# Five queues of the last attention put in another order, and ScalarE writing its transposed mask ahead of the score products

## What is computed

```python
# hidden_states, ssm_states: (8, 128, 256); 32 query heads, 8 key heads, head size 8
bias = concat([alibi, alibi], -1)            # slope[h] * (k - q)
mask = concat([0 <= q - k < 64, 0 <= q - k < 32], -1)
q = heads(concat([ssm_states, hidden_states], -1) @ Wq, 32)
k, v         = heads(hidden_states @ Wk, 8), heads(hidden_states @ Wv, 8)
ssm_k, ssm_v = heads(ssm_states @ Wsk, 8),   heads(ssm_states @ Wsv, 8)
kcat = concat([rep(ssm_k), rep(k)], 2); vcat = concat([rep(ssm_v), rep(v)], 2)
scores = q @ kcat.T / sqrt(8) + bias
scores = where(mask, scores, -inf)
o = softmax(scores) @ vcat
return o.reshape(B, T, 256) @ Wo
```

## Time and profile before

| | us |
|---|---|
| median of 3 runs | 1074.09 (1068.61 to 1078.88) |
| the profiled execution | 1076.21 |
| its span (first to last instruction) | 1074.40 |
| PE busy in the span | 988.4 (92%) |
| DVE, ACT busy | 639.3 (60%), 431.0 (40%) |
| stage E, t=9 to t=17 (from the first L800 to the last L1297) | 702.6 to 902.4 |

### The profile page before, as it was taken

One profiled execution on the slowest core, in us unless ns is written; L12 is line 12 of the kernel. 1 busy time (PEld: TensorE's weight loads), 2 busy tenths in 40 slices (PEclk: granted clock), 3 DMA queues, 4 the chain that ended last, 5 costly groups with the idle time before them and its releaser, 6 DMA issues.

```text
span 1074.4 us, 18672 instructions
## 1 busy us (share of the span) xinstructions
PE 988.4 (92%) x6076; PEld 775.9 (72%) x6076; DVE 639.3 (60%) x1450; ACT 431.0 (40%) x839; POOL 318.5 (30%) x534
## 2 busy tenths in 40 slices
PE   6999997979999999999999689867899998999994
PEld 5778885758888888888888335556677766688883
DVE  4676776535555555555556447665666673555555
ACT  4777783322323232232322123225555554422321
POOL 1132223224334434433444401110000004444331
PEclk9999997889999999999999779968999999999998
DMA  8000000553333333343330000011111101264511
GB/s 280 2 2 2 2 2 1 137 169 134 133 111 106 118 111 110 110 120 111 107 110 9 9 1 1 15 27 30 25 25 27 31 17 60 61 175 123 118 28 40
DMA packets 37354, 75.18 MB, mean 70 GB/s; under 512 B 7116, under 2 KB 18360, under 8 KB 37154
## 3 DMA queue, kind: packets, MB, share of 16 engines
q1 hardware_dynamic: 37006, 74.18, 23.8%
q0 software_dynamic: 288, 0.23, 0.2%
HBM read 67.21 MB, written 2.40 MB: 65 GB/s over the span
## 4 chain that ended last, share of the span: by engine, by line
PE 81%; DVE 6%; SPq 5%; issue 2%; DMA 2%; ACT 2%; POOL 1%; POOLq 0%; ACTq 0%; DVEq 0%
PE ps L1001 32%; PE ps L1018 15%; PE ps L413 4%; PE ps L638 4%; PE ps L502 3%; PE ps L420 3%; PE ps L867 2%; SPq L366 2%; SPq L322 2%; PE ps L494 2%; PE ps L533 2%; PE ps L755 1%; PE ps L805 1%; PE ps L846 1%; PE ps L842 1%
## 5 line engine op out<-in xcount | busy, mean ns | idle before, releaser
L1001 PE MATMUL ps<-shared 128*128 128x512 f32 x1560 | 383.3, 395 | 7.8 <-POOL shared L1999 7.1
L1001 PEld LDWEIGHTS ps<-shared 128*128 128x128 f32 x1560 | 296.9, 191 | 74.1 <-issue 12.2
L1405 ACT ACTIVATE shared<-pT 128x512 fp32r<-128x512 f32 x130 | 82.2, 632 | 286.3 <-DVE pT L1830 286.3
L1997 POOL CAST shared<-wraw 128x512 fp32r<-128x512 f32 (+1 forms) x130 | 91.3, 703 | 312.5 <-PE ps L1018 279.8
L1833 DVE TENSOR_TENSOR al<-pT,shared 128x512 fp32r<-128x512 f32 x130 | 116.8, 899 | 93.4 <-ACT shared L1405 93.4
L1822 DVE TENSOR_TENSOR e<-e,ps 128x512 f32<-128x512 f32 x130 | 89.4, 688 | 136.0 <-PE ps L1001 132.4
L1018 PE MATMUL ps<-shared 128*128 128x512 f32 x520 | 160.4, 390 | 1.3 <-DVE al L1833 1.2
L1999 POOL TENSOR_TENSOR shared<-wraw,shared 128x512 fp32r<-128x512 f32 (+1 forms) x130 | 132.1, 1016 | 10.4
L1887 POOL TENSOR_SCALAR newton<-agg 128x1 f32<-128x1 f32 (+1 forms) x36 | 9.2, 255 | 385.4 <-DVE agg L1450 358.8
L1018 PEld LDWEIGHTS ps<-shared 128*128 128x128 f32 x520 | 97.5, 188 | 22.8 <-DVE al L1833 2.1
L1399 ACT ACTIVATE e<-ps 128x512 f32<-128x512 f32 x130 | 77.7, 598 | 83.3 <-PE ps L1001 83.2
(11 more groups left out here) (222 smaller groups left out, 1429.2 us busy)
## 6 DMA issues: line engine op xcount, KB each, us to landing
kbd<-combine_C SPq DMA_DIRECT2D x46, 512.0 KB
wraw<-in_C_w SPq DMA_DIRECT2D x48, 384.0 KB, 8.1
kbd<-combine_F SPq DMA_DIRECT2D x15, 512.0 KB
wraw<-in_F_w SPq DMA_DIRECT2D x17, 384.0 KB, 7.0
kbd<-kbd SPq DMA_DIRECT2D x96, 32.0 KB, 1.9
kT<-kbd SPq DMA_DIRECT2D x48, 32.0 KB, 1.9
c_ctx_t<-in_ctx_t SPq DMA_DIRECT2D x1, 1024.0 KB, 8.6
out<-c_x_rows SPq DMA_DIRECT2D x2, 512.0 KB, 3.0
```

The costliest lines, as they stand in the source:

```text
L1001: mm = pe.matmul(GU[t][s], w[u][:, (c * 2 + s) * P:(c * 2 + s + 1) * P], xx[:, c, t * HALF:(t + 1) * HALF], start=(i == 0), stop=(i == 5))
L1405: act.activation(ah[t][:, :], a2[t], ACT.Copy).then_inc(S("ah"), 1)
L1997: pool.tensor_copy(wh[u][:, lo:hi], wraw[k][:, lo:hi]).then_inc(S("m_wh"), 1)
```

## The change

Five things are done; no others.

1. **The mask.** For steps with k % 3 = 0 the mask matmul L835 is left out, but for the first (n = 0). Instead ACT, behind the exponential of such a step (n), waits for its completion and writes the mask into the same bank with a Copy (bf16 mask from SBUF to 128x512 of PSUM), for step n + 3; PE waits for this (E_preset) in place of the exponential. This is 31 matmuls less on PE and 31 activations more on ACT.
2. **PE's order.** `out_rows(ef, 0)` and `keys_values(ep)` in step 4, `out_rows(ef, 1)` in step 6 and `maxima_T(es, 0)` in step 7 now stand between scores and scores_T; `x_T` and `queries` go from step 2 to step 1, `out_rows` from 3 and 5 to 4 and 6, `out_T` and `values(ev, 0)` from 7 to 8, `out_project` from 8 to 9.
3. **ACT's order.** `high_maxima(ev, 1)` ahead of exps 0; `act_x` and `high_queries` from step 2 to 1; keys and values copies are split (steps 3 and 4); `high_maxima(es, 0)` from step 7 to 5, `out_T` from 7 to 6, `outputs(ev, 0)` from 7 to 8. Of the four masks two stay at the end (steps 10 and 11) and two go to steps 1 and 2 of the next iteration.
4. **DVE's order.** `normalized` from step 1 to 0, `masks(es, 2)` from 0 to 1, `masks(ep, 0)` from 10 to 7, `low_maxima(es, 0)` from 7 to 8.
5. **SP's order.** In an iteration: `qst[0]` high (4 DMAs), low (2), `qst[1]` low (2), `kT[0]` (3), `qst[1]` high (4), `maxima_rows(es, 0)` (2), `kT[1]` (3), `maxima_rows(es, 1)` (2). The number of DMAs is the same.

```diff
@@ SP @@
-                if ev is not None:
-                    maxima_rows(ev, 1)
                 if ep is not None:
-                    spread_queries(ep)
-                    spread_keys(ep)
+                    spread_queries(ep, 0, False)
+                    spread_queries(ep, 0, True)
+                    spread_queries(ep, 1, True)
+                    spread_keys(ep, 0)
+                    spread_queries(ep, 1, False)
                 if es is not None:
                     maxima_rows(es, 0)
+                if ep is not None:
+                    spread_keys(ep, 1)
+                if es is not None:
+                    maxima_rows(es, 1)
@@ @@
+        def preset(k):
+            return k % 3 == 0
+
+        def presets(n):
+
+            return sum(preset(m % STEPS) for m in range(n - 2))
@@ PE, scores_T @@
                 if n >= 3:
-                    pe.wait_ge(S("E_exp"), n - 2)
+                    if preset(k):
+                        pe.wait_ge(S("E_preset"), presets(n))
+                    else:
+                        pe.wait_ge(S("E_exp"), n - 2)
...
-                    pe.matmul(bank, ident16[:, :], bc(tmask[0][:, :], 1, 8), start=True, stop=False,
-                              skip_group_check=True)
+                    if n < 3 or not preset(k):
+                        pe.matmul(bank, ident16[:, :], bc(tmask[0][:, :], 1, 8), start=True, stop=False,
+                                  skip_group_check=True)
@@ PE, the loop over steps @@
                     if es is not None:
                         scores(es, k)
+                    if k == 4 and ef is not None:
+                        out_rows(ef, 0)
+                    if k == 4 and ep is not None:
+                        keys_values(ep)
+                    if k == 6 and ef is not None:
+                        out_rows(ef, 1)
+                    if k == 7 and es is not None:
+                        maxima_T(es, 0)
                     if ev is not None:
                         scores_T(ev, k)
...
+                    if k == 1 and el is not None:
+                        x_T(el)
+                    if k == 1 and ep is not None:
+                        queries(ep)
                     if k == 2 and do is not None:
                         linear_project(do)
...
+                    if k == 8 and ef is not None:
+                        out_T(ef)
+                    if k == 8 and ev is not None:
                         values(ev, 0)
...
+                    if k == 9 and ef is not None:
                         out_project(ef)
@@ ACT, exps @@
                 act.activation(PRING[n % 8], TRING[n % 3], ACT.Exp, scale=scale).then_inc(S("E_exp"), 1)
+                if preset(k) and n + 3 < B * STEPS:
+
+                    act.wait_ge(S("E_exp"), n + 1)
+                    if k % 3 == 0:
+                        mask, bank = bc(tmask[0][:, :], 1, 8), TRING[0].rearrange("p (h q) -> p h q", h=8)
...
+                    act.activation(bank, mask, ACT.Copy).then_inc(S("E_preset"), 1)
@@ ACT, the loop over steps @@
+                    if k == 0 and ev is not None:
+                        high_maxima(ev, 1)
                     if ev is not None:
                         exps(ev, k)
...
+                    if k == 1 and ep is not None:
+                        high_queries(ep)
+                    if k in (1, 2) and es is not None and es > 0:
+                        masks(es, k + 1)
...
+                    if k == 3 and ep is not None:
+                        high_keys(ep)
                     if k == 4 and ep is not None:
-                        high_keys_and_values(ep)
+                        values_copy(ep)
+                    if k == 5 and es is not None:
+                        high_maxima(es, 0)
+                    if k == 6 and ef is not None:
+                        out_T(ef)
+                    if k == 8 and ev is not None:
                         outputs(ev, 0)
...
-                    if k >= 8 and ep is not None:
-                        masks(ep, k - 8)
+                    if k >= 10 and ep is not None:
+                        masks(ep, k - 10)
@@ DVE, the loop over steps @@
+                    if k == 0 and el is not None:
+                        normalized("E", el)
...
+                    if k == 1 and es is not None:
+                        masks(es, 2)
...
+                    if k == 7 and ep is not None:
+                        masks(ep, 0)
+                    if k == 8 and es is not None:
                         low_maxima(es, 0)
```

More of the change, by code:

```diff
@@ L353, in _, with spread_queries, spread_keys @@
             moe_loads(sp, "C")
[L355 to L369, removed]
+            def spread_queries(b, t, low):
+                if b > 0:
+                    sp.wait_ge(S("E_qma") if t else S("E_qm"), 4 * b if t else 2 * b)
+                sp.wait_ge(S("E_ql") if low else S("E_qh"), b + 1)
+                settle(sp)
+                for n in (1,) if low else (0, 2):
+                    to = qst[t][32 * n:32 * n + 32].rearrange("p (h o x) -> p h o x", h=2, o=2)
+                    for o in range(2):
+                        r = 64 * o + 32 * t
+                        sp.dma_start(to[:, :, o],
+                                     (ql if low else qh)[r:r + 32].bitcast(F32).rearrange("p (h x) -> p h x", h=2))\
+                          .then_inc(S(f"E_q{t}st"), 16)
+            def spread_keys(b, t):
                 if b >= 3:
@@ L375, in spread_keys @@
                     settle(sp)
-                    for t in range(2):
-                        sp.dma_start(ring(b)[1][t][32 * n:32 * n + 32].bitcast(F32),
-                                     part[32 * t:32 * t + 32].bitcast(F32)).then_inc(S(f"E_k{t}st"), 16)
+                    sp.dma_start(ring(b)[1][t][32 * n:32 * n + 32].bitcast(F32),
+                                 part[32 * t:32 * t + 32].bitcast(F32)).then_inc(S(f"E_k{t}st"), 16)
             def maxima_rows(b, r):
@@ L841, in scores_T @@
                     g = g0 + k % 3 - 1
-                    pe.matmul(bank, ident16[:, :],
-                              bc(tmask[1][:, :].rearrange("p (n q) -> p n q", n=2), 2, 4), start=True, stop=False,
-                              skip_group_check=True)
+                    if n < 3 or not preset(k):
+                        pe.matmul(bank, ident16[:, :],
+                                  bc(tmask[1][:, :].rearrange("p (n q) -> p n q", n=2), 2, 4), start=True, stop=False,
+                                  skip_group_check=True)
                     for i in range(2):
@@ L1723, in dve_linear_cross @@
                         low_maxima(ev, 1)
+                    if k == 0 and el is not None:
+                        normalized("E", el)
                     if k == 1 and t == B + 1:
                         normalized("D", t - 4)
[L1726 to L1727 removed]
+                    if k == 1 and es is not None:
+                        masks(es, 2)
+                    if k == 2 and ep is not None:
+                        low_queries(ep)
                     if k == 4 and ef is not None:
@@ L1731, in dve_linear_cross @@
                         dve_stats(dve, "D", do, do % 2)
-                    if k == 0 and es is not None:
-                        masks(es, 2)
-                    if k == 2 and ep is not None:
-                        low_queries(ep)
+                    if k == 4 and ep is not None:
+                        low_keys(ep)
                     if k == 6 and ef is not None:
                         normalize(ef, 1)
-                    if k == 4 and ep is not None:
-                        low_keys(ep)
-                    if k == 7 and es is not None:
+                    if k == 7 and ep is not None:
+                        masks(ep, 0)
+                    if k == 8 and es is not None:
                         low_maxima(es, 0)
@@ L1745, in dve_linear_cross @@
                         residual(ef)
-                    if k == 10 and ep is not None:
-                        masks(ep, 0)
             choose = Router(dve, "E")
```

45 lines of the change are left out of this document (12 added, 33 removed).

## The result

| | before | after |
|---|---|---|
| median beside each other, us | 1075.4 (4 runs, 1068.61 to 1078.88) | 1043.89 (4 runs, 1041.3 to 1045.09) |
| a second time, on another occasion | 1077.13 (11 runs) | 1048.62 (6 runs) |
| the profiled execution's span | 1074.4 | 1042.4 |
| from the first `queries` of stage E to the last exponential | 215.25 | 186.95 |

The changed kernel is faster: the ratio is 0.9711, 95% interval 0.9659 to 0.9764; the second time 0.9743 (0.9709 to 0.9776). Forecast was 1045.7, range 1038 to 1059.

What follows compares the result with a forecast made beforehand. Bound: a circle from PE through keys_values, low_keys and DVE back to PE, 22.25 us an iteration. Gains 6.0 (t=9) + 19.35 (t=10 to t=15) + 3.0 (t=16) = 28.4 off 1076.2 give 1047.8, median 1045.7; range 1038 to 1059.

Steps and rivals of the forecast that it cites:

- The circle: Steady iteration: PE to keys_values, on to low_keys, DVE's work, back to PE; 22.25 us before, 20.1 after.
- crossings: Steady iterations: 0.2 us added for small unseen crossings between engines, making 20.3 us an iteration.
- PE's work: Steady iterations: four mask matmuls fewer, 0.9 us, take PE's work from 20.1 to 19.2 us, below the circle.
- The steps in between: Within an iteration: keys_values at 7.6 us, SP's start 6.0, maxima's second issue 18.0, landed 19.9; PE's gap about 0.7.
- The write on ACT: ACT's 31 mask writes: 0.62 us each plus 0.10 for waits, 2.9 us an iteration, hidden.
- The rival that short gaps lower it: Seven iterations: the clock falls all the same, 1.2 us each, 8.4 us less gain, 1054 us; chance 0.15.
- The price of a fall: Iterations with PE's clock at the lower level for a part: about 1.2 us each, expected to go.
- t=9: First iteration: DVE's and PE's idle times, 7.3 us, go; new waits return 1.3; gain 6.0, bounds 4 and 7.
- t=16 and t=17: Last iterations: t=16 gains 3.0 us, bounds 1.5 and 3.5; t=17 and the tail 0, within 1.
- SP's queue: Steady iterations: SP's switches cost more, maxima land 2.4 us later, 1.5 more an iteration, 1055 us; chance 0.12.
- Only the masks count: Steady iterations: the circle keeps its length and only 7.2 us of masks is gained, 1067 us; chance 0.08.
- Slower: Steady iterations: ACT becomes the bound through costlier writes, up to 24.0 + 0.9 us an iteration, 1087 us; chance 0.05.

Runs made afterwards that it cites:

- e7: Changed kernel with ACT's values copy next to the keys copy (step 3), ahead of exponential 4: 1041.87 us, ratio 0.9703 to before.
- e5: Changed kernel with DVE's masks(ep, 0) back in step 10 and low_maxima(es, 0) back in step 7: 1061.5 us, ratio 0.9847 to before.
- e1: Changed kernel with all masks on PE again (ACT writes none), all new orders kept: 1055.09 us, ratio 0.9788 to before.
- e2: Kernel before with ACT's mask writes alone, every order as before: 1080.79 us, ratio 1.0026 to before.
- e4: Changed kernel with SP's old order, except kT[0]'s three DMAs come ahead of kT[1]'s: 1050.48 us, ratio 0.9791 to before.
- e3: Changed kernel, but ACT writes each mask twice, the second write waiting for the first: 1048.1 us, ratio 0.9737 to before.
- e6: Changed kernel with linear_z ahead of the masks of batch 0 on ACT: 1043.25 us, ratio 0.9679 to before.
- r_before: The kernel before, unchanged, run a second time for its profile: stage 215.36 us, against 215.25 in the first profile.
- e8: Changed kernel with the moves of e6 and e7 together: 1039.53 us, ratio 0.9674 to before; a second time 1034.87 us, ratio 0.9619.

## Why the prediction was right, point by point

**The circle was the bound, and its new length was right.** The sum was 11.45 to low_keys, 8.50 in DVE, 0.14 back to PE: 20.1, with 0.2 added for crossings. Measured: 11.40 + 8.69 = 20.09. The 0.2 for crossings wasn't needed, and t=10 and t=11 took 19.84 and 19.82; from that the six iterations gained 21.1 instead of 19.35. e7 tests the circle from the other side: 0.78 off it is 0.77 off the iteration. e5 shows the same by adding to it.

**PE's work.** It was put at 20.1, less four masks of 0.23: 19.2. PE's busy time went from 20.00 to 19.04, but a mask was worth 0.15 (e1) or 0.13 (e2 against before at the same clock, 20.00 to 19.48); so the masks make only 0.5 to 0.6 of it, and the rest came with the changed orders. As PE was not the bound, the error did not reach the forecast.

**The steps in between.** keys_values was put at 7.6 (7.51), SP's start at 6.0 (5.93), the maxima's second issue at 18.0 (17.5), PE's gap at 0.7 and put down to DVE's reduce (0.65, L1702). The landing counts by e4's row, 1.91 behind the issue, so the maxima land at 19.4; PE wants them 0.5 into the next iteration. e4 shows what SP's order was worth: 0.5 to 1.0 an iteration.

**The write on ACT.** 0.62 was taken, 0.602 measured over 31. The estimate worked out from the Trainium skill, ScalarE: Activation LUTs, section "What ACT_TABLE_LOAD costs", was 0.61; the trace agrees. That it is hidden was argued before and is shown by e3.

**The clock.** It stays at 1.00 from t=11 through t=16. The rival that short gaps lower it did not come: PE has two gaps in t=13, 0.65 and 0.39, and in e4 three (0.66, 0.60, 0.39) at 1.00 too. The rule that I had set beside it (the Trainium skill, TensorE: Matmul & The Clock Gate, section "A second HAM failure mode: psum-queue depth-cycling", frequent micro-idles make the clock swing) is not borne out by gaps of this size here. Of the iterations t=12 to t=15 that begin behind a gap of 1.8 to 2.4, three of four were below 1.00 in the kernel before, three of four in e2 and two of four in e5. The price of a fall that the sum held, 1.2 us, was the smallest one: 1.6 at 0.93 and 3.1 at 0.86 in e5. What exactly sets off the fall stays open; no run varied the gap alone.

**t=9 was wrong.** The step was "queries now fit into the time in which PE waits for DVE's linear stage. Both idle times go, 7.3 us; ... Gain 6.0". DVE's 4.60 before low_queries and PE's 2.67 before t=10 did go. But I read only the two waits that I saw in the old trace, and not what SP's new order does to ACT's masks of batch 0, nor who is queued behind them. The masks start 14.55 us after the first `queries` instead of 12.59, and linear_z, the statistics, the linear stage and PE's second scores wait in a row behind them. Measured +0.9. Against that stood 3.9 us ahead of t=9 that I hadn't looked at, since I cut the kernel at the first scores: kT[0] is now complete before the last four query DMAs and before kT[1]. PE's wait for it was 6.88 before, is 5.34 in e4, where kT[0] comes ahead of kT[1] but behind all queries, and 2.93 in the changed kernel. Together -3.0 instead of -6.0. Two runs show the cause: with linear_z ahead of the masks (e6) t=9 takes 21.53 us, and with SP's old order (e4) 19.68, so that the other orders alone give 5.1 of the 6.0.

**t=16 and t=17.** -3.1 for a forecast of -3.0, with the clock at 1.00 instead of 0.91. In the tail I expected 0, within 1; it gained 1.05.

**The rivals.** The clock did not fall. SP's queue did not take over: the maxima's second issue comes at 17.5, and what ends PE's wait is DVE's reduce. "Only the masks count" is refuted by e2 and by 2.16 us an iteration at the same clock. "Slower" is refuted by e3; its price doesn't come out of its own sum either, since 8 us more over six iterations make 1084 for the profiled execution and 1082 for the median, not 1087.

So the total (28.3 for 28.4 in the stage) is closer than its parts, and that is luck: 3.0 too much in t=9 with its entry, against 1.75 too little in the iterations and 1.05 in the tail. And the median came below 1045.7 the first time and above it the second, by the chance length of what lies ahead of the stage.

**What the parts are worth**, each taken back alone from the changed kernel, by the stage: the mask's write 3.4, SP's order 2.7, DVE's mask and maxima 13.0 (of which some 6 for the clock). They leave 9.4 of 28.5 for PE's and ACT's orders, but what works only together is counted in each part or in none, so the prices need not add up; PE's and ACT's orders were not taken back in any run. Done alone, the write is worth 1.6 in the stage and nothing that a median shows.

## What to carry to other kernels

Find the circle between engines that sets a steady iteration and cost an edit by what it takes off that circle: a matmul saved elsewhere mostly makes a wait longer, and an instruction moved from the circle's end into a wait inside it is worth nearly its full length (here 1.1 of 1.22 us, and the clock fell less often besides). When a queue of DMAs is put in another order, follow each transfer that now comes later to the instruction that waits for it and to all that is queued behind this on its engine, in the first, irregular iteration above all. Compare the touched stage inside the profiles and not only the whole time, and start it at the first work that the moved instructions can reach.

## What the runs showed of the hardware

- One kernel's time ahead of stage E differs by 4.5 to 6.2 us between executions (682.07 and 686.56 for before). In the first 300 us the granted clock was 0.95 in the profile of before, 0.97 in r_before; from 600 to 680 it was 0.83 and 0.89. The stage itself repeats to 0.35 us.
- Iterations of the same instructions took 21.2, 22.8 and 24.3 us at a granted clock of 1.00, 0.93 and 0.86 (e5): a fall to the lower of the two levels (1.2 of 2.4 GHz) for a part of the iteration costs 1.6 to 3.1 us, more than any single edit here changes an iteration at full clock (1.1).
- The same four matmuls (L703, 256 columns) took 1.36 us to the start of the next one in e6 and 0.68 in e8, in stretches with a granted clock of 0.61 and 0.79.
- An activation that copies a bf16 mask from SBUF to 128x512 of PSUM took 0.602 us (31 of them, 0.600 to 0.603). Three DMAs in a row on SP take 1.84 us (kT, x3), and the last issue of the maxima came 1.91 us before the product that waits for it (e4).
- Where it falls is repeated by a second execution of the same kernel: t=13 alone at 1.00, its neighbours at 0.93.
